# Three query and key projections of batch 1 moved ahead of the first attention pass, with the first pass's other units spread out

## The reference, cut to what matters

```python
# x: (4, 512, 512) float32; 32 query heads, 8 key/value heads, head width 16
def attn(x):                                   # x is already layer-normed here
    q, k, v = heads(x @ Wq), heads(x @ Wk), heads(x @ Wv)
    q = q * cos + rotate_half(q) * sin
    k = k * cos + rotate_half(k) * sin
    att = einsum('bhgqd,bhkd->bhgqk', grouped(q), k) / sqrt(16)     # 4 query heads per key head
    probs = softmax(where(causal, att, -inf))
    return merge(einsum('bhgqk,bhkd->bhgqd', probs, v)) @ Wo
x = x + attn(layernorm(x))
n = layernorm(x)
x = x + (silu(n @ W_gate.T) * (n @ W_up.T)) @ W_down.T
```

## Time and profile before

| what | value |
|---|---|
| median of three runs | 773.08 us |
| the profiled execution | 772.49 us, its span 770.8 us |
| PE busy | 737.8 us of the span (96%) |
| DVE, ACT, POOL busy | 445.2, 333.8, 241.9 us |
| first, second, third pass (by the first `scores_t`) | from 53.36, 133.79, 213.87 us |
| mean granted PE clock | 0.989 |

### The profile page before, as it was taken

The page is one execution under the profiler, slowest core; times in us unless marked ns, Lnnn a source line. Parts: engine busy times, 40 slices in busy tenths (PEclk is TensorE's granted clock), DMA queues, the critical chain, the costliest instruction groups (busy, mean ns, idle before and its releaser), DMA issues.

```text
span 770.8 us, 12186 instructions
## 1 busy us (share of the span) xinstructions
PE 737.8 (96%) x4149; PEld 502.4 (65%) x4164; DVE 445.2 (58%) x1136; ACT 333.8 (43%) x646; POOL 241.9 (31%) x467
## 2 busy tenths in 40 slices
PE   5889999999999999998999999999999999999998
PEld 4645444554444543443788888888888888788886
DVE  6897789888987889997355443234232333231212
ACT  4337678767976778667343222111121111111111
POOL 4257885688658774556000000000000000000000
PEclk9869999999999999999999999999999999999999
DMA  7337587234434455530592103211014020030001
GB/s 272 98 108 250 182 280 239 67 87 125 119 96 130 142 179 151 160 99 29 174 310 72 42 14 118 88 59 51 14 48 142 27 82 27 0 110 1 1 0 55
DMA packets 74759, 81.86 MB, mean 106 GB/s; under 512 B 8864, under 2 KB 58528, under 8 KB 74496
## 3 DMA queue, kind: packets, MB, share of 16 engines
q1 hardware_dynamic: 73408, 79.98, 32.7%
q10 hardware_dynamic: 1296, 1.18, 0.5%
HBM read 57.02 MB, written 33.36 MB: 117 GB/s over the span
## 4 chain that ended last, share of the span: by engine, by line
PE 51%; DVE 0%; issue 0%; DVEq 0%
PE bank L1578 35%; PE ps_y L1630 15%; PE bank L1617 1%; DVE x_in L1560 0%; DVEq L1559 0%
## 5 line engine op out<-in xcount | busy, mean ns | idle before, releaser
L929 DVE CUSTOM_DVE_ANT_0 ps_s<-ps_s,mask_row 128x512 f32<-128x512 f32 (+1 forms) x360 | 192.1, 583 | 36.6 <-PE ps_s L1188 34.0
L792 ACT ACTIVATE probs<-ps_t 128x512 f32<-128x512 f32 (+1 forms) x352 | 178.2, 560 | 68.6 <-PE ps_t L1222 68.3
L1535 DVE TENSOR_TENSOR h<-h,bank 128x512 f32<-128x512 f32 (+1 forms) x44 | 30.2, 687 | 212.8 <-PE bank L1578 211.6
L1188 PE MATMUL ps_s<-k_rows,q_rows 96*128 96x256 bf16 (+3 forms) x512 | 141.0, 309 | 5.7 <-DVE m_raw L929 2.9
L1222 PE MATMUL ps_t<-q_rows,k_rows 98*128 98x512 bf16 (+1 forms) x352 | 126.9, 364 | 4.4 <-DMA q_rows<-m_t 2.4
L240 POOL TENSOR_TENSOR var_eps<-mean_var,eps 128x1 f32<-128x1 f32 x16 | 3.0, 189 | 281.7 <-DVE mean_var L235 281.7
L1473 ACT ACTIVATE h<-bank 128x512 f32<-128x512 f32 (+1 forms) x44 | 26.3, 597 | 145.2 <-PE bank L1578 145.2
L1235 PE MATMUL ps_o<-probs,v_ones 128*32 128x512 f32 (+3 forms) x1024 | 82.0, 438 | 3.4 <-POOL probs L693 1.1
L693 POOL TENSOR_SCALAR_AFFINE_SELECT probs<-probs 128x512 f32<-128x512 f32 x128 | 83.4, 652 | 0.0
L1479 ACT CAST h_hi<-h 128x512 fp32r<-128x512 f32 (+1 forms) x44 | 27.3, 620 | 126.5 <-DVE h L1535 126.5
L1188 PEld LDWEIGHTS ps_s<-k_rows,q_rows 96*128 96x128 bf16 x512 | 48.2, 100 | 47.8 <-DVE m_raw L929 22.3
(11 more groups left out here) (167 smaller groups left out, 1366.1 us busy)
## 6 DMA issues: line engine op xcount, KB each, us to landing
scratch_o<-o_sb SPq DMA_DIRECT2D x31, 256.0 KB, 2.4
q_rows<-scratch_q_parts SPq DMA_DIRECT2D x32, 192.0 KB
x_in<-in_x SPq DMA_DIRECT2D x16, 256.0 KB, 4.0
q_rows<-scratch_q_parts SPq DMA_DIRECT2D x32, 128.0 KB
o_in<-scratch_o SPq DMA_DIRECT2D x64, 64.0 KB
inverse<-scratch_inverse SPq DMA_DIRECT2D x64, 64.0 KB
x_res<-in_x SPq DMA_DIRECT2D x16, 256.0 KB, 2.7
out<-x_in SPq DMA_DIRECT2D x16, 256.0 KB, 2.1
```

The lines of the kernel that those rows point to most:

```text
L792: nc.scalar.activation(probs[:, g % 2, heads * u:heads * (u + 1), CHUNK_AT[c]:CHUNK_AT[c + 1]], ps_t[:, pos % S_BANKS, 0:heads * CHUNK_N[c ...
L929: taken = nc.vector.tensor_tensor_reduce(out=head, in0=head, in1=mask_row[:, T - width:T], scale=1.0, scalar=LOWEST, op0=ALU.add, op1=ALU. ...
L1188: mm = nc.tensor.matmul(bank[:, place], q_rows[r][0:ROWS, j, P * q:P * (q + 1)], k_rows[r][0:ROWS, 0:width], start=(place == 0), stop=(mas ...
L1535: nc.vector.tensor_tensor(h[0:m, r], h[0:m, r], bank[units["up", f] % BANKS][0:m, :], ALU.mult).then_inc(h_ready, 1)
```

## The change

Three units of batch 1 (R0, R1, R2) are made in the lead-in, each piece behind a pair of score heads, in a bank of `ps_t`, in `ps_d` and in `ps_o`. ACT copies them out there, and POOL does the four rotation steps of the keys ahead of the first pass. The transposed maxima of group 0 go into a bank of `ps_t`, with semaphores of their own. In the first pass R3, R4 and V remain, with a piece in every second gap, and the remaining 16 rotation steps stand one to a slot. `LO_SLOT` changes for all passes; `LAST_O` moves one copy from slot 30 to slot 29.

```diff
-        steps = [gap(first + n) for n in range(1 if kind in "TU" else 4)]
+        steps = [gap(first + n) for n in ((0,) if kind in "TU" else range(0, 4 * apart[0], apart[0]) if apart else range(4))]
...
-UNITS_IN = [QKV_UNITS + NEXT_T] * (B - 2) + [QKV_UNITS, LAST_UNITS]
+AHEAD = 3
+AHEAD_AT = {(0, 1, 1): (0, 0), (0, 1, 3): (0, 1), (0, 2, 1): (0, 2), (0, 2, 3): (0, 3),
...
+FIRST_UNITS = [("R", 3, 2, 2), ("R", 4, 11, 2), ("V", 0, 19, 2), ("U", 0, 27)]
+UNITS_IN = [FIRST_UNITS + NEXT_T] + [QKV_UNITS + NEXT_T] * (B - 3) + [QKV_UNITS, LAST_UNITS]
+PRE_DENSE = KC + N_ROPE + 2 + KC + AHEAD
...
-ROPE_SLOT = [3, 4, 5, 6, 7, 8, 10, 10, 11, 12, 13, 14, 15, 17, 18, 19, 21, 22, 23, 25]
+FIRST_ROPE = [None] * ROPE_AHEAD + [1, 2, 3, 5, 6, 7, 9, 10, 13, 14, 15, 17, 18, 19, 21, 22]
...
-LO_SLOT = {7: 0, 13: 1, 16: 2, 23: 3, 27: 4}
+LO_SLOT = [{1: 0, 9: 1, 13: 2, 21: 3, 25: 4}] + [{7: 0, 13: 1, 14: 2, 22: 3, 26: 4}] * (B - 2)
...
-LAST_O = {26: 5, 30: 6}
+LAST_O = {26: 5, 29: 6}
...
+            for s in range(ROPE_AHEAD):
+                rotate(1, s)
+                if s in REST_STEP:
+                    rotated_low(1, REST_STEP.index(s))
...
                 if n == 0:
-                    act.wait_ge(dense_ready, PRE_UNITS)
-                    nc.scalar.copy(m_t[0][:], ps_d[rows, 0:P]).then_inc(dense_evacuated, 1)
+                    act.wait_ge(first_max_ready, 1)
+                    nc.scalar.copy(m_t[0][:], ps_t[rows, 0, 0:P]).then_inc(first_max_evacuated, 1)
...
             store_rotated(act, 0, 3)
+            raw_rows(1, 0, r_unit(1, 0))
             rotated_top(0, 4)
             first_max_high()
             max_evacuate(0)
             store_rotated(act, 0, 4)
+            for k in range(1, AHEAD):
+                raw_rows(1, k, r_unit(1, k))
...
+                if n == 0 and c == 0 and j == 0:
+                    pe.wait_ge(dense_evacuated, PRE_DENSE - AHEAD + 1)
...
                 if c == 0:
-                    if positive(n):
+                    if n == 0:
+                        pe.wait_ge(dense_evacuated, PRE_DENSE)
+                    else:
                         pe.wait_ge(o_evacuated, n)
...
                         scores(0, n, i, j)
+                        if (n, i, j) in AHEAD_AT:
+                            k, piece = AHEAD_AT[n, i, j]
+                            dense(1, "R", k, r_unit(1, k), piece)
```

More of the change, by code:

```diff
@@ L66, in pieces_at @@
     at, done = {}, {}
-    for place, (kind, k, first) in enumerate(units):
-        steps = [gap(first + n) for n in range(1 if kind in "TU" else 4)]
+    for place, (kind, k, first, *apart) in enumerate(units):
+        steps = [gap(first + n) for n in ((0,) if kind in "TU" else range(0, 4 * apart[0], apart[0]) if apart else range(4))]
         for piece in range(4):
@@ L78 @@
               ("T", 3, 39)]
-UNITS_IN = [QKV_UNITS + NEXT_T] * (B - 2) + [QKV_UNITS, LAST_UNITS]
-PRE_DENSE = KC + N_ROPE + 2 + KC
-PRE_UNITS = PRE_DENSE + 1
+AHEAD = 3
+AHEAD_AT = {(0, 1, 1): (0, 0), (0, 1, 3): (0, 1), (0, 2, 1): (0, 2), (0, 2, 3): (0, 3),
+            (1, 0, 1): (1, 0), (1, 0, 3): (1, 1), (1, 1, 1): (1, 2), (1, 1, 3): (1, 3),
+            (1, 2, 1): (2, 0), (1, 2, 3): (2, 1), (1, 3, 1): (2, 2), (1, 3, 3): (2, 3)}
+FIRST_UNITS = [("R", 3, 2, 2), ("R", 4, 11, 2), ("V", 0, 19, 2), ("U", 0, 27)]
+UNITS_IN = [FIRST_UNITS + NEXT_T] + [QKV_UNITS + NEXT_T] * (B - 3) + [QKV_UNITS, LAST_UNITS]
+PRE_DENSE = KC + N_ROPE + 2 + KC + AHEAD
 PRE_BANKS = 1 + S_BANKS
-UNIT0 = [PRE_UNITS + sum(len(u) for u in UNITS_IN[:b]) for b in range(B)]
-ROPE_SLOT = [3, 4, 5, 6, 7, 8, 10, 10, 11, 12, 13, 14, 15, 17, 18, 19, 21, 22, 23, 25]
+UNIT0 = [PRE_DENSE + sum(len(u) for u in UNITS_IN[:b]) for b in range(B)]
+ROPE_AHEAD = 4
+FIRST_ROPE = [None] * ROPE_AHEAD + [1, 2, 3, 5, 6, 7, 9, 10, 13, 14, 15, 17, 18, 19, 21, 22]
+ROPE_SLOT = [FIRST_ROPE] + [[3, 4, 5, 6, 7, 8, 10, 10, 11, 12, 13, 14, 15, 17, 18, 19, 21, 22, 23, 25]] * (B - 2)
 KEY_STEPS, PAIR_STEPS = 4, 8
@@ L312, in dense_bank @@
         def dense_bank(unit):
-            if isinstance(unit, int) and unit < PRE_DENSE and unit % PRE_BANKS:
+            if unit == PRE_DENSE - 1:
+                return ps_o[:]
+            if unit < PRE_DENSE and unit % PRE_BANKS:
                 return ps_t[:, unit % PRE_BANKS - 1]
@@ L346, in phase_1 @@
         mask_added = sem("mask_added")
+        first_max_ready = sem("first_max_ready")
+        first_max_evacuated = sem("first_max_evacuated")
         max_done = sem("max_done")
@@ L381, in w_unit, with v_unit @@
             return LAST_UNIT0 + t
+        def v_unit(b):
+            return UNIT0[b - 1] + len(UNITS_IN[b - 1]) - KC - 1 if 0 < b < B - 1 else UNIT0[b] - 1 if b else KC + N_ROPE + 1
         def r_unit(b, k):
-            return UNIT0[b - 1] + k if b else KC + k
+            if b == 0:
+                return KC + k
+            if b == 1:
+                return PRE_DENSE - AHEAD + k
+            return UNIT0[b - 1] + k
         def rest_done(engine, b, k):
@@ L461, in stage_max @@
                 if n == 0:
-                    sp.wait_ge(dense_evacuated, PRE_UNITS)
+                    sp.wait_ge(first_max_evacuated, 1)
                 else:
@@ L521, in iteration @@
                         load_x(b + 3)
-                    if has_next and slot - 1 in LO_SLOT:
-                        store_rotated(sp, b + 1, LO_SLOT[slot - 1])
+                    if has_next and slot - 1 in LO_SLOT[b]:
+                        store_rotated(sp, b + 1, LO_SLOT[b][slot - 1])
                     if i == 0 and n + 3 < GROUPS:
@@ L708, in iteration @@
                     if has_next:
-                        for s, at in enumerate(ROPE_SLOT):
+                        for s, at in enumerate(ROPE_SLOT[b]):
                             if at == slot:
@@ L826, in iteration @@
                         max_evacuate(n + 1)
-                    if i == PV_EVACUATE and n >= 1 and (has_next or slot not in LAST_O):
+                    if i == PV_EVACUATE and n >= 1 and (has_next or g - 1 not in LAST_O.values()):
                         o_evacuate(b, g - 1)
                         if g == 0:
-                            v_place(b, UNIT0[b - 1] + 6 if b else KC + N_ROPE + 1)
+                            v_place(b, v_unit(b))
                     for u in range(GROUP // HEADS_OF[i]):
@@ L835, in iteration @@
                                 dense_read(b, *done[slot, j])
-                    if has_next and slot in LO_SLOT:
-                        rotated_top(b + 1, LO_SLOT[slot])
+                    if has_next and slot in LO_SLOT[b]:
+                        rotated_top(b + 1, LO_SLOT[b][slot])
                     if not has_next and (slot - CTX_HI) % TT == 0 and 0 <= slot - CTX_HI < TT * TT:
@@ L998, in next_work @@
                     if slot in NEXT_XT:
-                        work.append(lambda: xt_low(b + 2, NEXT_XT[slot], UNIT0[b] + len(QKV_UNITS) + NEXT_XT[slot]))
+                        work.append(lambda: xt_low(b + 2, NEXT_XT[slot], UNIT0[b + 1] - KC + NEXT_XT[slot]))
                 return work
@@ L1200, in transposed_max @@
                 if n == 0:
-                    bank_free(PRE_UNITS - 1, 0)
-                    to, ready = ps_d[:], dense_ready
+                    pe.wait_ge(dense_evacuated, KC + N_ROPE + 2 + KC)
+                    to, ready = ps_t[:, 0], first_max_ready
                 else:
@@ L1269, in _ @@
                         mm.then_inc(dense_ready, 1)
-            for unit in range(KC, PRE_DENSE):
+            for unit in range(KC, PRE_DENSE - AHEAD):
                 kind, k, of = ("R", unit - KC, 0) if unit < KC + N_ROPE else (
```

## The result

The changed kernel takes 777.49 us (median of 8 runs, 773.78 to 779.83), the kernel before 773.13 beside it: ratio 1.0067, 95% interval 1.0051 to 1.0084. It is slower by 4.4 us by the medians and 5.2 us by the ratio; I had forecast 769.8, faster.

A forecast was written before the change was run, and what follows sets the result against it. The prediction took PE to bound the kernel. Against the profiled 772.49 us it summed -8.5 + 7.7 + 0.2 - 1.3 - 1.1 = -3.0 to 769.5, and predicted a median of 769.8 us, range 766.5 to 774.5.

The forecast's parts named there:

- What bounds the kernel: Whole kernel: PE is busy 96% of the span, so a pass lasts as long as PE's work in it.
- First pass, -8.5: First pass: twelve pieces leave PE and two waits go, less a charge for DVE; 8.5 us gained, bounds 4.5 and 9.8.
- +0.2: Start of the first pass: ACT's copy of R2 delays its first exponential; 0.2 us charged, bounds 0 and 0.6.
- 1.0 us for waits on `m_t`: First pass: PE's two waits go because stores of rotated tiles now come behind `stage_max`; 1.0 us gained.
- Lead-in, +7.7: Lead-in: twelve added pieces, a new stall of some 1.5 us and a clock fall make it 7.7 us longer.
- Second and third pass, -1.3: Later passes: the fourth tile's earlier cut removes PE's wait for `m_t`; 1.3 us gained, bounds 0 and 1.4.
- End of phase 1, -1.1: End of phase 1: DVE's earlier `ps_o` copy lets the last values product start sooner; 1.1 us gained, bounds 0 and 1.2.
- B: First pass: DVE becomes the bound, pass 75.9 us, total 773.5; chance 0.28 together with the middle form of C.
- C: Lead-in: the clock stays at half throughout, costing 17.1 us instead of 7.7, total 778.9; chance 0.12.
- D: Lead-in: the clock stays full after the stall, costing 6.3 us, total 768.1; chance 0.15.
- Sum: Whole kernel: all terms net to -3.0 us against the profiled execution, 769.5, with a predicted median of 769.8.

The follow-up runs named there:

- e1: Changed kernel with the twelve weight copies in the second pass instead of the first: 773.38 us, ratio 1.0007 to the kernel before.
- e6: Changed kernel with each of the twelve first-pass weight copies moving only eight rows there, the rest in the second pass: 773.6 us, ratio 1.0014 to before.
- e10: Kernel before with the weight copies in the second pass and the changed `LAST_O`, `m_t` left on SP: 770.95 us, ratio 0.9977.
- e9: Changed kernel with weight copies in the second pass, key copies behind the maxima, old later-pass `LO_SLOT`, `m_t` on SP: 769.15 us, ratio 0.996 to before.
- e3: Changed kernel with ACT's three key-unit copies moved behind the first maxima: 773.86 us, ratio 1.002 to the kernel before.
- e4: Kernel before with only the changed `LO_SLOT` of the later passes and the changed `LAST_O`: 771.34 us, ratio 0.9975.
- e2: Kernel before with the twelve weight copies in the second pass instead of the first: 771.38 us, ratio 0.9983.
- e7: Changed kernel, weight copies in second pass, key copies behind maxima, old later-pass `LO_SLOT`, ACT issuing all `m_t` but group 0's: 770.11 us, ratio 0.9955 to before.
- e5: Changed kernel with the first pass's `m_t` transfers issued by ACT right behind its cast: 777.98 us, ratio 1.0062 to the kernel before.
- e8: Kernel before with weight copies in the second pass, the changed `LAST_O`, and ACT issuing all `m_t` but group 0's: 773.21 us, ratio 0.9998.

## Why the prediction was wrong

- *What bounds the kernel*: "work taken out of it shortens it, as long as DVE does not become the next bound". This is the sentence that failed. The row under it had the third candidate in its last columns: the DMA share 0.69 in the first pass, 0.34 in the second. I gave it no price and no rival. The runs showed in its place waits for DMA of 4.9 us and 3.4 us of half clock behind them; with the weight copies gone (e1) or thin (e6) the pass is 72.7 or 72.9 us.
- *First pass, -8.5*: measured -1.5, the step that made the forecast wrong. The piece was sized right: PE's busy time in e1 is 8.2 us less than before for twelve pieces, 0.68 each (8.9 us, 0.74 each, between e10 and e9, whose matmul records are complete), and e1's pass is 7.7 us shorter against the 8.3 that the two terms -8.5 and +0.2 made. The 1.0 us for waits on `m_t` had the wrong sign: I read the earlier trace rows as a matter of order in SP's queue, and they grew from 1.0 to 4.0 us with the row loads' 0.9 beside them. e6 shows that they come of the bytes of the copies, which stood 7 us and more ahead of a late `m_t` before and 4.1 to 4.8 us ahead of it now. The half clock from 80.7 to 84.1 us came on top.
- *Lead-in, +7.7*: right, +8.0. The first `scores_t` came at 60.40 for 61.1 forecast, DVE's wait 1.21 us, PE's pauses 1.57 us, clock half for some 3.4 us behind them. The clock fell behind the stall as I had let it; e3 adds the counter-test, no pause and no fall. Short pauses alone don't settle it, though: PE stands 0.8 us in e9's lead-in, and the clock stays full from 40 us on. Counted from the first scores the stall ended after 12.4 us (12.7 forecast), and the rest took 8.4 (7.9), though the clock rose 3.8 us earlier than I had assumed. Two errors met here: ACT's high part was ready 10.5 us behind the first scores (49.87 to 50.09), where I had 11.6, and DVE's low part took 1.22 us, where I had 0.3. So the size is in part luck. That the place of the key copies makes the stall is what e3 confirms; that most of PE's 1.20 us would be DVE's low part beside POOL's step, I had not seen.
- *Second and third pass, -1.3*: wrong sign. The cut moved by one exponential, 0.5 us, not 1.5, since it passed only one exponential in ACT's queue. The store was issued 0.5 us earlier in its group, but the load at 283.97 now stands behind it, so `m_t` left 6.07 us into the group where it had left 5.95, and PE waits 1.21 us for 1.28. The new wait of 0.61 at 272.23 is for an `m_t` issued 7.76 us into its group (7.60 before) that took 2.95 us to its use, where 2.43 had sufficed without a wait; why it lands later stays open. e4 shows the tables alone: +0.9.
- *End of phase 1, -1.1*: right. From the last `scores_t` to the last values product it is 0.31 us where it was 1.49, so -1.2, here and in e4. The last pass is 1.6 us shorter; the other 0.4 lie earlier in it, and most of it (0.3) is in e2 too, which has the old tables.
- *Rivals*: B (DVE bound) is refuted, e1 runs its pass in 72.7 us, under the 75.9 of B, with DVE at 89% and no wait on it above 0.3 us. C did not come. D's condition, a clock that stays full, is what e3, e7 and e9 have.
- *Sum*: -3.0 forecast, +4.6 in the profiled pair; the first pass is 6.8 of the 7.6 between them, the second and third 1.9, the lead-in 0.3, and the end and the earlier start give back 1.4. One slip stands in the sum itself: 769.5 and the 0.6 between execution and median make 770.1, not 769.8, which changes nothing here.

## What to carry to other kernels

Before work is taken out of a stretch bound by one engine, set everything else in it against the shorter length, the DMA bytes too: 0.69 of the DMA engines in 80 us would be 0.76 in 73. Look at distances as well as at the mean: what mattered here is that a small transfer on which each group waits came to be issued before the bulk copies ahead of it had landed. Bulk copies with no deadline belong in a stretch with a low DMA share, and there they cost something too, 1.7 us of the 6.2 here. A wait of a few tenths for a small transfer can be a sign of load and not of order: in e2, with the order on SP as it was and the copies gone, the first pass has none. A copy put into an engine's queue ahead of the first thing that another engine waits for delays that, and it can also make two other instructions coincide; here the clock fell behind the pause besides.

## What the runs showed of the hardware

- An 8 KB transfer issued 4.1 to 4.8 us behind two copies of 688 KB was used 3.7 to 5.1 us after its issue (after), and PE waited for three of the four. Issued 7.0 and 11.6 us behind such copies, it was used after 3.2 and 2.9 us (before). Behind copies of eight rows at the same distance, 2.6 and 2.8 us sufficed without a wait (e6). It was 7.7 us in one case from ACT's queue, at 326 GB/s (e5). The mean of the pass does not tell these apart (228 GB/s before, 230 after, 137 in e6).
- A DMA issue holds ACT for 0.62 to 0.67 us, the first of each run for 1.22 (e5, e7, e8), and the exponentials wait behind it.
- A subtraction of two SBUF tiles on DVE (128x16) took 1.22 us beside a two-input step of POOL in four traces, and 0.17 or 0.18 us with POOL idle in eight.
- The same lead-in rises to full clock at different times from one execution to the next: near 45 us in e3, before 40 in e9. Their lead-ins are 18.45 and 16.84 us, so a difference of two profiles is no measure of an edit there.
